# Ranking edges for a counting sort on one core: key rows fetched repeated and compared on VectorE in place of transposes and products on TensorE

## The reference, cut to what matters

```
edge_index = jnp.stack([src, dst])
x = _layernorm(x + _L0_gnn_ref(x, edge_index, edge_attr_3, ...))     # spline convolutions
x = _layernorm(x + _L1_gnn_ref(x, edge_index, ...))                  # three attention layers
x = _layernorm(x + _L2_gnn_ref(x, node_vec1, edge_index, ...))
x = _layernorm(x + _L3_gnn_ref(x, edge_index, 3))

# within _L0_gnn_ref:
row, col = (edge_index[0], edge_index[1])
out = jax.ops.segment_sum(msg, row, num_segments=N)
```

## Time and profile before

| | |
|---|---|
| runs, median | 10791.19 us |
| profiled execution, span | 11739.9 us |
| the same, less the median | 948.7 us |
| busy: PE, DVE, ACT, POOL | 3519.0, 5446.7, 2549.9, 6010.3 us |
| ranking loop, POOL's first to last scatter | 203.6 to 1553.2 us |
| POOL busy in it | 779.0 us |

### The profile page before, as it was taken

The page is one execution under the profiler, slowest core; times in us unless marked ns, Lnnn a source line. Parts: engine busy times, 40 slices in busy tenths (PEclk is TensorE's granted clock), DMA queues, the critical chain, the costliest instruction groups (busy, mean ns, idle before and its releaser), DMA issues. The chain is left out here.

```text
span 11739.9 us, 84883 instructions
## 1 busy us (share of the span) xinstructions
PE 3519.0 (30%) x18873; PEld 2268.8 (19%) x18929; DVE 5446.7 (46%) x8000; ACT 2549.9 (22%) x3835; POOL 6010.3 (51%) x6000
## 2 busy tenths in 40 slices
PE   4333300366334444343332100010000200035787
PEld 3222200243111111232222100010000100023554
DVE  5223268344666666456776322232222577861201
ACT  0222225244233333211111011111111244420000
POOL 1555557300566666535666577757776566640000
PEclk8555555588555555555555555555555555558899
DMA  7000012299799999625555111111111133328798
GB/s 297 2 2 2 2 55 104 92 387 385 293 371 367 368 370 365 259 61 143 143 145 152 39 35 34 32 25 39 32 33 32 43 97 95 99 70 308 286 411 355
DMA packets 582790, 1887.73 MB, mean 161 GB/s; under 512 B 253627, under 2 KB 315490, under 8 KB 552065
## 3 DMA queue, kind: packets, MB, share of 16 engines
q0 software_dynamic: 305264, 762.32, 21.5%
q1 hardware_dynamic: 234592, 722.30, 15.9%
q10 hardware_dynamic: 42784, 401.43, 8.2%
HBM read 1170.21 MB, written 715.38 MB: 161 GB/s over the span
## 5 line engine op out<-in xcount | busy, mean ns | idle before, releaser
L2308 POOL DMA_INDIRECT ring<-tab_gat,at x2352 | 2350.7, 999 | 924.7 <-issue 848.1
L729 POOL DMA_INDIRECT ring<-z_stn,at x784 | 763.2, 973 | 1315.7 <-POOLq L736 786.7
L574 POOL DMA_INDIRECT sorted<-rows,at x784 | 779.0, 994 | 771.9 <-POOLq L572 537.4
L1552 PE MATMUL pair_acc<-pair_x_w,pair_cell 32*112 32x384 f32 (+1 forms) x1120 | 780.7, 879 | 1124.3 <-remote 476.1
L1879 POOL DMA_INDIRECT ring<-z_conv,at x784 | 805.7, 1028 | 599.4 <-POOLq L1877 367.6
L2887 PE MATMUL acc<-spot,ones 128*128 128x128 f32 x6 | 2.3, 486 | 3443.8 <-PEq L2878 1192.7
L1299 PE MATMUL acc<-tile,parts 128*96 128x448 f16 (+1 forms) x3430 | 726.7, 361 | 255.1 <-DVE parts L1223 138.9
L2419 DVE COPY peak<-peak 128x6 f32<-128x6 f32 x112 | 19.9, 178 | 1570.2 <-DMA ring<-tab_gat,at 1422.3
L2887 PEld LDWEIGHTS acc<-spot,ones 128*128 128x128 f32 x6 | 1.5, 311 | 3444.5 <-issue 3444.5
L1552 PEld LDWEIGHTS pair_acc<-pair_x_w,pair_cell 32*112 32x112 f32 x1120 | 317.1, 295 | 1586.9 <-issue 1580.3
L2343 ACT ACTIVATE weights_bank<-arg 128x168 f32<-128x168 f32 (+1 forms) x112 | 31.2, 279 | 2416.6 <-issue 1994.3
(11 more groups left out here) (538 smaller groups left out, 10030.9 us busy)
## 6 DMA issues: line engine op xcount, KB each, us to landing
tile<-adj SPq DMA_DIRECT2D x490, 784.0 KB, 21.4
z_stn<-block ACTq DMA_DIRECT2D x98, 2400.0 KB
z_conv<-pair_block ACTq DMA_DIRECT2D x224, 700.0 KB
run_gat<-out_rows SPq DMA_DIRECT2D x56, 1596.0 KB
adj<-zero SPq DMA_DIRECT2D x49, 1568.0 KB
run_basis<-out_rows SPq DMA_DIRECT2D x28, 1750.0 KB
ring<-tab_gat,at POOLq DMA_INDIRECT x2352
run_gat<-out_rows SPq DMA_DIRECT2D x56, 672.0 KB
```

The lines of the kernel that those rows point to most:

```text
L574: g.indirect_dma_start(out=dest, out_offset=bass.IndirectOffsetOnAxis(ap=at[b][:, k:k + 1], axis=0), in_=rows[b][:, k, :], in_offset=None) ...
L729: g.indirect_dma_start(out=view(bufs[b], k), out_offset=None, in_=table, in_offset=bass.IndirectOffsetOnAxis(ap=at[n][b][:, k:k + 1], axis ...
L1552: last = pe.matmul(self.acc[g][0:self.nodes, n, 0:(hi - lo) * self.fo], self.cell[:, :], cols, start=True, stop=True)
L2308: g.indirect_dma_start(out=ring[b][:, k, :], out_offset=None, in_=tab_gat, in_offset=bass.IndirectOffsetOnAxis(ap=at[b][:, k:k + 1], axis= ...
```

## The change

For each tile the equal keys in front of an edge are now counted on VectorE. In `stage_load`, VectorE also makes the low digits of the rows as bf16, and SP writes the keys (`key_rows`) and the low digits (`low_rows`) of all edges to memory, one row of 1792 for each tile: 15 DMAs each, and the stage ends when they have landed. In the ranking loop ScalarE, which has nothing else to do there, fetches for each tile the row of keys (f32, 7168 bytes) and of low digits (bf16, 3584 bytes) repeated over all 128 partitions: 917.5 and 458.8 KB. `make` waits for them. It then builds `hot_lo` in the layout of the first loop, `hot_hi` from the bf16 digits, `lo_rows` by one comparison of the fetched low digits with the partition's number, and for each of the 14 columns one `scalar_tensor_tensor` that compares 128 fetched keys with the edge's own, masks those that come later, and sums the rest into `within`. TensorE keeps the 14 matmuls for the table and has 14 for the look-up, with both parts of `first` side by side (98 columns in place of three times 49). VectorE multiplies and sums 1372 in place of 686 elements, and adds `within` when it writes the places.

```
+                    for d, tile in ((key_rows, rawf[0]), (low_rows, low_b)):
+                        for s_ in range(ST):
+                            sp.dma_start(d[0:SW, s_ * P:(s_ + 1) * P]...,
+                                         tile[s_ * per:(s_ + 1) * per, :]...).then_inc(c.sem, 16)
...
+                    sp.wait_ge(c.sem, n)
...
+                    v.tensor_scalar(low_i[:, :], raw[0][:, :], P - 1, None, ALU.bitwise_and)
...
+                    v.tensor_copy(low_b[:, :], low_i[:, :]).then_inc(sem("rows_split"), 1)
...
                     def make(b, step):
-                        v.tensor_copy(keys.unsqueeze(3), digits[:, :, :, bass.ds(step, 1)]).then_inc(dve_step, 1)
-                        v.wait_ge(dve_step, 1)
-                        v.sem_inc(dve_step, -1)
-                        v.tensor_tensor(hot_lo[b][:, :, :], keys[:, 0, :].unsqueeze(2).to_broadcast([P, ST, P]),
-                                        iota[:, 0:P].unsqueeze(1).to_broadcast([P, ST, P]), ALU.is_equal)
-                        v.tensor_tensor(hot_hi[b][:, :, :], keys[:, 1, :].unsqueeze(2).to_broadcast([P, ST, NT]),
-                                        iota[:, 0:NT].unsqueeze(1).to_broadcast([P, ST, NT]), ALU.is_equal).then_inc(dve_step, 1)
...
+                        v.wait_ge(sem(f"tile_in{b}"), 32)
+                        v.sem_inc(sem(f"tile_in{b}"), -32)
+                        v.tensor_copy(keys[b][:, :].unsqueeze(2), full[:, :, bass.ds(step, 1)]).then_inc(dve_step, 1)
+                        v.tensor_tensor(keys_inside(hot_lo[b]), short[:, 0, bass.ds(step, 1), :].to_broadcast([P, P, ST]),
+                                        number[:, :, :], ALU.is_equal)
+                        v.tensor_tensor(hot_hi[b][:, :, :], short[:, 1, bass.ds(step, 1), :].rearrange("p o s -> p s o").to_broadcast([P, ST, NT]),
+                                        iota[:, 0:NT].unsqueeze(1).to_broadcast([P, ST, NT]), ALU.is_equal)
+                        v.tensor_scalar(flat(lo_rows[b]), flat(low_all[b]), lane[:, 0:1], None, ALU.is_equal).then_inc(sem("hot_made"), 1)
...
+                        for j in range(ST):
+                            last = v.scalar_tensor_tensor(same[:, j, :], key_all[b][:, j, :], keys[b][:, j:j + 1], before[:, :],
+                                                          ALU.is_equal, ALU.mult, accum_out=within[b][:, j:j + 1])
+                        last.then_inc(sem(f"ring_free{b}"), 1)
...
-                            v.tensor_tensor(halves(prod), wide(found), halves(hot_hi[b]), ALU.mult).then_inc(dve_step, 1)
+                            v.tensor_tensor(prod[:, :, :, :], found.rearrange("p j (m k) -> p j m k", m=2),
+                                            hot_hi[b][:, :, :].unsqueeze(2).to_broadcast([P, ST, 2, NT]), ALU.mult).then_inc(dve_step, 1)
...
-                            v.tensor_scalar(at[b][:, :], rank[:, :], MIDDLE, None, ALU.add).then_inc(dve_step, 1)
+                            v.scalar_tensor_tensor(at[b][:, :], rank[:, :], MIDDLE, within[b][:, :], ALU.add, ALU.add).then_inc(sem(f"ranked{b}"), 1)
...
+                    def fetch(b, step):
+                        a.dma_start(key_all[b][:, :, :].rearrange("p j e -> p (j e)"),
+                                    key_rows[bass.ds(step, 1), :].rearrange("o e -> (o e)").partition_broadcast(P)).then_inc(sem(f"tile_in{b}"), 16)
+                        a.dma_start(low_all[b][:, :, :].rearrange("p j e -> p (j e)"),
+                                    low_rows[bass.ds(step, 1), :].rearrange("o e -> (o e)").partition_broadcast(P)).then_inc(sem(f"tile_in{b}"), 16)
...
+                            a.wait_ge(sem(f"ring_free{b}"), 1)
+                            a.sem_inc(sem(f"ring_free{b}"), -1)
+                            fetch(b, it * 2 + b + 2)
...
-                            turn(b, *units[0])
-                            for n, (lo, hi) in enumerate(units):
-                                take("lo_rows_ready")
...
                             for j in range(ST):
-                                for k in range(2):
-                                    pe.matmul(cell(found, j), lo_rows[:, j, :], parts[b][:, k, j, :], start=(k == 0), stop=False)
-                                last = pe.matmul(cell(found, j), earlier[:, j, :], hot_hi[b][:, j, :], start=False, stop=True)
+                                last = pe.matmul(found[:, j, :], lo_rows[b][:, j, :], parts[b][:, j, :, :].rearrange("p m k -> p (m k)"),
+                                                 start=True, stop=True)
```

More of the change, by code:

```diff
@@ L45, in gnn_stack_kernel @@
     SW = J // ST
-    UN = 4
     QR, QK = 112, 7
@@ L316, in stage_rank @@
                 digit_i = sb(st, "digit_i", [P, J], I32)
[L317 to L318 removed]
+                full = sb(st, "full", [P, ST, SW + 1])
+                short = sb(st, "short_b", [P, 2, SW + 1, ST], BF16)
                 number = sb(st, "number_b", [P, P, ST], BF16)
[L320 removed]
                 none = sb(st, "none_b", [P, P], BF16)
[L322 removed]
+                before = sb(st, "before", [P, P])
                 hot_lo = [sb(st, f"hot_lo{b}", [P, ST, P], BF16) for b in range(2)]
                 hot_hi = [sb(st, f"hot_hi{b}", [P, ST, NT], BF16) for b in range(2)]
[L325 to L326 removed]
+                lo_rows = [sb(st, f"lo_rows{b}", [P, ST, P], BF16) for b in range(2)]
+                low_all = [sb(st, f"low_all{b}", [P, ST, P], BF16) for b in range(2)]
+                key_all = [sb(st, f"key_all{b}", [P, ST, P]) for b in range(2)]
+                keys = [sb(st, f"keys{b}", [P, ST]) for b in range(2)]
+                same = sb(st, "same", [P, ST, P], BF16)
+                within = [sb(st, f"within{b}", [P, ST]) for b in range(2)]
                 first = [sb(st, f"first{b}", [P, ST, NT]) for b in range(2)]
[L328 to L329 removed]
+                parts = [sb(st, f"parts{b}", [P, ST, 2, NT], F16) for b in range(2)]
+                prod = sb(st, "prod", [P, ST, 2, NT])
                 counted_ = sb(st, "counted", [P, ST, NT])
@@ L355, in halves, with columns, flat @@
                     return tile[:, :, :].rearrange("p (h j) k -> p h (j k)", h=2)
+                def columns(j, b):
+                    return keys_inside(hot_lo[b])[:, :, j]
+                def flat(tile):
+                    return tile[:, :, :].rearrange("p j k -> p (j k)")
                 @block.vector
                 def _(v):
-                    v.memset(digits[:, :, :, SW:SW + 1], 0.0)
+                    v.memset(full[:, :, SW:SW + 1], 0.0)
+                    v.memset(short[:, :, SW:SW + 1, :], 0.0)
                     v.tensor_copy(number[:, :, :], iota[:, 0:P].unsqueeze(2).to_broadcast([P, P, ST]))
@@ L439, in _ @@
                     v.sem_inc(dve_step, -1)
-                    v.scalar_tensor_tensor(first[0][:, 0, :], run[:, :], -MIDDLE, cell(found, 0), ALU.add, ALU.add).then_inc(dve_step, 1)
+                    v.scalar_tensor_tensor(first[0][:, 0, :], run[:, :], -MIDDLE, found[:, 0, 0:NT], ALU.add, ALU.add).then_inc(dve_step, 1)
                     v.wait_ge(dve_step, 1)
@@ new lines, in _ @@
+                    a.wait_ge(counted("edge_load").sem, counted("edge_load").base)
+                    for b in range(2):
+                        fetch(b, b)
+                    with a.Fori(0, steps) as it:
+                        for b in range(2):
+                            a.wait_ge(sem(f"ring_free{b}"), 1)
+                            a.sem_inc(sem(f"ring_free{b}"), -1)
+                            fetch(b, it * 2 + b + 2)
+                    a.wait_ge(sem("ring_free0"), 1)
+                    a.sem_inc(sem("ring_free0"), -1)
```

90 lines of the change are left out of this document (28 added, 62 removed).

## The result

18 runs of the changed kernel have a median of 10822.95 us (10805.09 to 10855.19), 18 of the kernel before 10786.31 (10761.94 to 10825.71). The ratio is 1.0031 (95% interval 1.0023 to 1.0040): 36.6 us slower, where +69 was forecast. The direction was right and the size too large. One execution among the experiments, of before_gate, took 11626.23 us where its ten others took 10753 to 10777; its ratio is without that one.

What follows compares the result with a forecast made beforehand. The runs' ranking loop was taken as bound by POOL's scatters at 18.1 us a tile. Removed work 0, POOL's waits +54 and the start +15 gave 10791 + 69 = 10860 us, range 10780 to 11050.

Steps and rivals of the forecast that it cites:

- POOL is the bound, VectorE's tile hides: Ranking loop: POOL's scatters set 18.1 us a tile; VectorE's 15.1 hides, TensorE's and ScalarE's removed work is worth 0.
- The profile's 949 us are not in the runs: Profiled execution 11739.9 us against the runs' 10791.19; 320 of the 949 us were placed in the ranking loop's stalls.
- the recording makes them: Ranking loop: dense matmul records, some 7 per us, hold TensorE's stream and semaphores back once a buffer is full.
- the span falls by 250: Changed kernel's profiled span falls by 250 us, to about 11490, and the runs don't fall.
- POOL's waits, 54 × 1.0 = +54: Ranking loop: new VectorE instructions with SBUF inputs hold POOL's scatters at their start, 1.0 us a tile, 54 tiles.
- The start, +15: Before the steady ranking loop: load stage 5 us later, fetches delaying SP's list +10, less 1.5; bounds 0 and 30.
- the change touches that, the load stage before it, and nothing behind it: Reading of the stretches: only the ranking loop, 186 to 1560 us, and the load stage are affected.
- Signs: Changed profile: scatters every 1.27 to 1.37 us, tiles 18 to 20, VectorE idle 3 to 4, first steady scatter 274.
- Real stalls: Rival: TensorE is held up in the runs too, so the change removes 320 us; 10540 us, 12%.
- Waits don't grow: Rival: POOL's scatter starts fall between VectorE's instructions or settle in step; only the start's 15, 10806 us, 15%.
- VectorE the bound: Rival: sums at 0.5 us and lo_rows at 1.95 make VectorE's ranking tile 20 us; 10909 us, 12%.
- chain not let through: Rival: POOL's scatter can't slip between VectorE's closely following instructions, 54 × 5 + 15 = 285; 11076 us, 11%.

Runs made afterwards that it cites:

- before_gate: Kernel before with SP's loads of constants put behind the waits for the scatters; ratio 0.9984 against the kernel before.
- before_extra: Kernel before with a fifteenth scatter in each tile of the ranking loop; ratio 1.0063 against the kernel before, +68 us.
- after_twice: Changed kernel with each of a tile's fourteen sums made twice; ratio 1.0050 against the kernel before.
- before_again: Kernel before, unchanged, profiled a second time; span 10789.9 us.
- after: The changed kernel itself, with its profile, against the kernel before; median 10822.95 us, ratio 1.0031.
- before_load: Kernel before with only the changed kernel's load stage, its rows written and never read; ratio 1.0015 against the kernel before, +16 us.
- after_psum: Changed kernel with one input of the hot_lo and hot_hi comparisons and of the sums in PSUM; ratio 1.0001 against the kernel before.
- after_busy: Changed kernel with 50 filler matmuls more per tile on TensorE behind the look-up; ratio 1.0035 against the kernel before.

## Why the forecast had the sign and not the size

- *POOL is the bound, VectorE's tile hides (13.35 us, 15.1 forecast), TensorE's and ScalarE's work was worth 0.* Right for POOL and VectorE (before_extra, after_twice). That the other two were worth 0 follows from before_again's tiles, 18.32 us against POOL's own 18.1; no run takes their work away alone.
- *The profile's 949 us are not in the runs.* Right; *the recording makes them*, and *the span falls by 250*: wrong. I built a mechanism from one execution, and took its 949 us for a distance between a profile and its own time; in before_again and after the span is 1.8 us under the time of the same execution. The span fell by 928 against that one and rose by 22 against a sound one.
- *POOL's waits, 54 × 1.0 = +54.* The mechanism held down to the instruction; the size was 0.64, 34.6 us, because starts and instructions move in step (`hot_lo` 0.23 for my 0.36, `lo_rows` 0.05 for 0.21) and because `split`'s share fell from 0.30 to 0.21.
- *The start, +15.* It was 31.5: the load stage 12.3 where I took 5 (30 issues of 0.7 us, not 0.5, from 24.2 us on in before_load, and the landing), the fetches some 20 where I took 10. The working didn't even give the 15: 41 − 34.7 + 1 is 7.3 and not 5 for the stage, and 5 + 10 − 1.5 is 13.5.
- 54 + 15 = 69 against 66.1 where the ranking ends: two misses, −19 and +17, that cancel by luck. The step that failed, and made the runs' figure wrong, is the one that bounded the change, "the change touches that, the load stage before it, and nothing behind it", which put everything behind the ranking at 0. The change takes 46 instructions out of ScalarE's program, and a later loop of 282 ceases to load its code anew at each turn: 15 to 24 us in the runs. With them, 66 − 20 = 46, still over the interval (25 to 43 us). A stretch of VectorE's work from L2999 at 8324.9 to L2455 at 9391.9 us in before_again is some 8 us shorter with the change (1058 to 1064 us in all eight profiles that have it, 1066 to 1069 in the six experiments on the kernel before and in before_again, with and without padding). With it the sum is 38, inside the interval; its cause stays open.
- *Signs.* Scatters every (813.7 + 232.8)/784 = 1.33 us, tiles of 18.96 us and sums at 0.27 us came as forecast; VectorE's idle time (5.9 us a tile, not 3 to 4) and the first steady scatter (290.0, not 274) did not.
- *Rivals.* Real stalls: out. Waits don't grow: out as a mechanism, though its 10806 us was 17 from the 10823 measured and my 10860 was 37. VectorE the bound, chain not let through: out.

## What to carry to other kernels

Profile twice before building on a wait that no semaphore explains and compare several profiles before crediting 10 or 20 us of a far stage to an edit: here 19 us between two of them were chance. When work moves to VectorE beside a busy POOL, price what POOL loses at each start, and keep one input in PSUM where GpSimd is the bound: to forget it cost 32 us here, and one line that took an input out of PSUM in the kernel before cost 74. And an edit that shortens one engine's program moves all its later loops against the pieces in which code is loaded; count packets of the instruction queue per stage before crediting a far-off gain, or loss, to the edit.

## What the hardware showed that I had not expected

- The execution at 11739.9 us was 949 us longer, and not everywhere: 307 of them lie in the ranking, none in the `z_stn` stage, where PE is busy two thirds of the time (551 us, 550 in before_again), and none from 9400 us of before_again on. What made it long stays open.
- A `scalar_tensor_tensor` of 128 f32 elements with a sum steps by 0.27 us, with its mask in SBUF and in PSUM alike (292.69, 292.96, 293.23 in after_psum):

```profile
292.69 0.34 DVE L424 SCALAR_TENSOR_TENSOR same<-key_all,keys,fixed 128x128 bf16<-128x128 f32 x1
...
292.96 0.34 DVE L424 SCALAR_TENSOR_TENSOR same<-key_all,keys,fixed 128x128 bf16<-128x128 f32 x1
```

  The Trainium skill (Vector Engine (DVE) Microarchitecture Reference, Points that are easy to get wrong) has half rate for two SBUF sources that aren't bf16; the estimate by it, 128 × 2/0.96 = 267 ns, fits the first, but with one source in PSUM it did not get faster.
- TensorE's granted clock stayed at 1.0 for the whole ranking once its matmuls fell from 4872 to 1568, and its fall in after_busy did not move the runs by more than the interval.
